# A two-layer gated cross-attention and mixture-of-experts kernel: unit slots of the second layer, the order before the first expert tile, and the place of a bias sum

## What is computed

```python
x = x + tanh(g_xattn[0]) * L0_xattn(layernorm(x), ctx)   # 16 heads of 16, 375 keys, clip, softmax, + bo
x = x + tanh(g_ffn[0])   * L0_ffn(layernorm(x))          # 8 experts, top 2, gelu; times three matrix exponentials; gated mix
x = x + tanh(g_xattn[1]) * L1_xattn(layernorm(x), ctx)   # 16 heads of 64, 371 keys, plus an attention over 4 more keys; LoRA weights
x = x + tanh(g_ffn[1])   * L1_ffn(layernorm(x))          # shared expert + 8 experts, top 2, silu gate
```

## Time and profile before

| | us |
|---|---|
| median of 3 runs | 988.82 (978.87, 988.82, 989.82) |
| the profiled execution | 985.29 |
| its span in the profile | 983.5 |
| PE, DVE, ACT, POOL busy | 861.8, 668.6, 497.5, 500.8 |
| mean granted TensorE clock | 0.945 of full speed |

### The profile page before, as it was taken

The page is one execution under the profiler, slowest core; times in us unless marked ns, Lnnn a source line. Parts: engine busy times, 40 slices in busy tenths (PEclk is TensorE's granted clock), DMA queues, the critical chain, the costliest instruction groups (busy, mean ns, idle before and its releaser), DMA issues.

```text
span 983.5 us, 21996 instructions
## 1 busy us (share of the span) xinstructions
PE 861.8 (88%) x7463; PEld 682.4 (69%) x7463; DVE 668.6 (68%) x1532; ACT 497.5 (51%) x1058; POOL 500.8 (51%) x525
## 2 busy tenths in 40 slices
PE   1789999999897999977679899898998976999994
PEld 1579988888775877755456677676776766666663
DVE  6487766666875768776657677777787777743333
ACT  4365555555533645542356655656556553334441
POOL 4779999998512324211126745556455562124420
PEclk9899999999856999998799999999999998999997
DMA  5423333347382225447002222222221248911114
GB/s 174 158 87 95 107 113 107 116 149 240 124 293 78 65 81 156 136 124 262 29 23 87 66 66 87 66 86 74 76 86 63 66 139 270 351 39 55 59 45 129
DMA packets 81485, 113.73 MB, mean 116 GB/s; under 512 B 7786, under 2 KB 60083, under 8 KB 81284
## 3 DMA queue, kind: packets, MB, share of 16 engines
q1 hardware_dynamic: 75556, 99.92, 32.0%
q0 software_dynamic: 4032, 11.02, 3.7%
q10 hardware_dynamic: 1824, 1.84, 0.5%
HBM read 75.78 MB, written 36.96 MB: 115 GB/s over the span
## 4 chain that ended last, share of the span: by engine, by line
PE 51%; DVE 15%; POOL 13%; issue 8%; ACT 6%; DMA 6%; SPq 0%; ACTq 0%; DVEq 0%; POOLq 0%
PE sp L892 5%; PE tp L906 5%; PE pb L850 5%; POOL Z L1296 4%; PE sp L2053 4%; PE tp L2053 3%; POOL Z L1304 3%; PE pb L2083 3%; POOL qz L1373 3%; PE tp L2278 3%; PE pb L871 3%; PE pb L844 3%; PE sp L1909 2%; ACT ST L1041 2%; PE pb L1927 2%
## 5 line engine op out<-in xcount | busy, mean ns | idle before, releaser
L1048 ACT ACTIVATE ST<-tp 125x672 f32<-125x672 f32 (+1 forms) x128 | 93.4, 730 | 156.3 <-PE tp L906 156.3
L892 PE MATMUL sp<-KT,qz 128*112 128x375 f16 (+1 forms) x768 | 118.5, 333 | 32.7 <-ACT ST L1041 21.2
L1296 POOL TENSOR_SCALAR Z<-Z 128x512 f32<-128x512 f32 x94 | 140.9, 1499 | 4.4 <-DMA Z<-in_moe 4.2
L906 PEld LDWEIGHTS tp<-identf,ST 112*125 112x125 f32 x768 | 98.5, 191 | 24.2 <-issue 14.3
L906 PE MATMUL tp<-identf,ST 112*125 112x112 f32 x768 | 111.6, 282 | 4.3 <-POOL ST L1404 3.3
L1304 POOL TENSOR_TENSOR Z<-Z 128x512 f16<-128x512 f32 x94 | 111.0, 1181 | 6.2
L892 PEld LDWEIGHTS sp<-KT,qz 128*112 128x112 f16 (+1 forms) x768 | 66.9, 129 | 63.7 <-ACT ST L1041 29.5
L1857 POOL DMA_INDIRECT back<-ST,slot_row x42 | 43.6, 1039 | 127.8 <-ACT ST L1967 67.1
L1851 POOL DMA_INDIRECT ST<-rows,slot_from x42 | 41.5, 988 | 93.6 <-DVE slot_weight L1836 52.7
L1177 DVE TENSOR_SCALAR_CACHE_REDUCE ST<-sp 112x375 f32<-112x375 f32 x128 | 65.0, 545 | 35.2 <-PE sp L892 35.1
L1404 POOL TENSOR_TENSOR ST<-pn,sums 112x8 f32<-112x8 f32 x64 | 12.9, 201 | 142.6 <-ACT ST L1041 142.6
(11 more groups left out here) (352 smaller groups left out, 1993.1 us busy)
## 6 DMA issues: line engine op xcount, KB each, us to landing
Z<-in_moe SPq DMA_DIRECT2D x86, 256.0 KB, 3.1
cut_scratch<-Z SPq DMA_DIRECT2D x86, 256.0 KB, 2.6
KT<-cut_scratch SPq DMA_DIRECT2D x16, 384.0 KB, 7.8
W<-cut_scratch SPq DMA_DIRECT2D x8, 512.0 KB, 5.6
W<-cut_scratch SPq DMA_DIRECT2D x32, 128.0 KB
W<-w_scratch SPq DMA_DIRECT2D x6, 512.0 KB, 8.8
V<-cut_scratch SPq DMA_DIRECT2D x8, 384.0 KB
own_scratch<-Z SPq DMA_DIRECT2D x8, 256.0 KB, 3.6
```

What stands on the lines that cost most here:

```text
L892: mm = pe.matmul(SB_[j][0:S, 0:L.keys], q, kT[bs % 2][qb][r, t, 0:L.keys], start=(n == 0), stop=(n == 2))
L906: mm = pe.transpose(TB_[j][0:CHUNK, c * S:(c + 1) * S], P_[:, st % 2, j, c * CHUNK:(c + 1) * CHUNK], identf[0:S, 0:S])
L1048: act.activation(PT[:, st % 2, :, 0, :] if l else PT0[:, st % 2, :, :], TP2[0:CHUNK, :, 0:NCH * S], ACT.Copy)\
L1296: pool.tensor_scalar(whole, whole, WS, None, ALU.mult).then_inc(s["cut_up"], 1)
```

## The change

- Layer 1's `at` becomes 0, 1, 2, ... 10, 12, ...: the second q unit goes from slot 2 to slot 1, each of the eight k units one slot earlier (3 to 10 become 2 to 9), the i unit from 11 to 10. The v units stay at 12, 13, 13, 14, 15, 15.
- `out_bias_gpsimd(0)` goes from the head of POOL's queue to behind `masks(1)`, and SP issues the two rows' transfers behind three of the late chunks.
- DVE before the first tile: `expm_first_vector`, then `bias_vector`, then `cut_x0_vector(0)`, then `expm_rest_vector` and `eyes_vector`.
- PE's transpose of the bias (`bias_turn_tensor`) is issued ahead of the last batch in `abel_tensor` and no longer after it.

```diff
-            at = dict(enumerate((0, 2, 3, 4, 5, 6, 7, 8, 9, 10, 11, 12, 13, 13, 14, 15, 15)))
+            at = dict(enumerate((0, 1, 2, 3, 4, 5, 6, 7, 8, 9, 10, 12, 13, 13, 14, 15, 15)))
...
-                out_bias_gpsimd(pool, 0)
                 masks(0, 0)
...
                         if b + 1 < B and n == pieces_by(b) + 2:
                             masks(b + 1, b + 1)
+                            if b == 0:
+                                out_bias_gpsimd(pool, 0)
...
+                if b == B - 1:
+                    bias_turn_tensor(pe)
...
-        def bias_tensor(pe):
-
+        def bias_turn_tensor(pe):
             pe.transpose(pb[0][0:E * NM, 0:128], b1[:, :, :].rearrange("p e m -> p (e m)"), identf[:, :])\
               .then_inc(s["bias_mm"], 1)
+
+        def bias_tensor(pe):
             pe.wait_ge(s["bias_set"], 1)
...
         def tiles0_vector(dve):
-            cut_x0_vector(dve, 0)
...
+            sp.wait_ge(s["chunk_lo"], 1)
+            chunks_sync(sp, NE, NE + 3)
             for l in range(2):
                 o = ROW[f"bo{l}"][0]
                 sp.dma_start(out_bias[:, l, :], a["rows"][0, o:o + C].partition_broadcast(S)).then_inc(s["w1_in"], 16)
-            sp.wait_ge(s["chunk_lo"], 1)
-            chunks_sync(sp, NE, NE + 3)
...
             owner_vector(dve, 0)
+            expm_first_vector(dve)
             bias_vector(dve)
-            expm_first_vector(dve)
+            cut_x0_vector(dve, 0)
             expm_rest_vector(dve)
```

## The result

| | median, us | ratio to the kernel before, 95% interval |
|---|---|---|
| before | 988.5 (978.9 to 996.0, 20 runs) | |
| after | 977.0 (972.4 to 985.3, 20 runs) | 0.989 [0.9871, 0.991] |

The changed kernel is 11.5 us faster by the medians, where 8.4 were forecast (980.4; range 972 to 990). Its profiled execution took 981.05 us, with a span of 979.3 and a mean granted clock of 0.936; the one of before took 985.29 at 0.945. So a difference of two whole spans says little here. I read stages from a mark at their start to a mark at their end, and compare whole times by medians and by the ratio only; the ratio gives 10.9 us. Some executions fall in a slower state and are left out of the ratios; one of them was profiled, the first of the kernel with both bias sums early, so that kernel is read from its second profile.

What follows compares the result with a forecast made beforehand. Layer 0's attention was bound by full PE and POOL, the stretch before the first tile by a chain of short steps. Terms -1.8 + 3.8 - 3.8 - 6.6 = -8.4 took the median 988.8 to 980.4 us; range 972 to 990.

Steps and rivals of the forecast that it cites:

- The bias sum leaves the start: Start of layer 0: without POOL's add, DVE's cut of WKV ends earlier and all behind it shifts, -1.8 us.
- It arrives in the first batch: Layer 0's first batch: DVE's 784-column cut waits for POOL's moved add, +3.8 us, bounds 0 and 4.5.
- My margin of 0.3 us: Layer 0's first batch: the add starts at about 52.8, DVE's 784-column cut 0.2 to 0.3 us after it.
- the add slips between the cuts: Rival, layer 0's first batch: the +3.8 falls away, so 976.6 us; chance 0.13.
- the two scalings: POOL's steps before the add, behind `masks(1)`: start at 50.8, take about 2 us.
- POOL's 6.5 us more: Layer 0, POOL's queue: 6.5 us more is covered by waits for q units, the longest shrinking to 2.5; cost 0.
- Before the first tile: Ahead of the first expert tile: DVE's new order and the early transpose start `up(0)` at 303.0 for 306.83, -3.8 us.
- the gather of 0.94 us: Before the first tile: a POOL gather beside L2308 in the old trace, read as showing no loss.
- The slots: Layer 1's seven batches: the q unit fills a wait, PE saves a k unit, -6.6 us, bounds 0 to -9.
- the t unit does not move: Layer 1's middle batch: the t unit stays at 636.39, so only one k unit, 0.80 us, is saved.
- start at 633.7 all the same: Layer 1's middle batch: `maxima(2)` on DVE can start at 633.7, with scores(2) at 632.3, 0.4 later.
- A mark that failed: Sign of being right: `up(0)` some 2 us earlier than 306.83 in absolute time.

Runs made afterwards that it cites:

- the move alone: The kernel before with only layer 0's bias sum moved behind `masks(1)`, with SP's order of transfers; ratio 1.0017 [0.9985, 1.0048].
- the two-source version: The changed kernel with the three scalings L2311 written as a product less its own source, two SBUF sources for one; ratio 0.9877 [0.9828, 0.9927].
- the early second sum: The changed kernel with the first bias sum ahead of `masks(2)` and layer 1's ahead of its batches; to the kernel before 0.9817, in a second series 0.9842.
- The separate ratios: The kernel before with one part changed each: slots alone 0.9899, the bias sum's move alone 1.0017, the order before the first tile alone 0.9941.

## Why the prediction was right, point by point

The forecast of a gain below 2% and the range held; 980.4 was 3.4 us too high.

*The bias sum leaves the start, -1.8.* Right: `masks(0)` starts at 28.32 us where it started at 29.96, 1.6 earlier.

*It arrives in the first batch, +3.8.* Right in mechanism, slightly over in size: the add began first, the cut grew by 4.11 - 0.95 = 3.16 us in the changed kernel and by 4.09 in the move alone. My margin of 0.3 us between the starts of add and cut was 1.2 and 0.3 in these two profiles. In the third with the sum in this place the cut came 1.8 us before the add, so there the rival "the add slips between the cuts" came half true: the 784-column cut slipped by and the next was held by 2.57 us. That two of three went my way is in part luck. The steps before it were off too: I had the two scalings start at 50.8, and they started at 48.20, directly behind `masks(1)`. The place was a bad one: ahead of `masks(2)` in POOL's queue the sum held no cut.

*POOL's 6.5 us more, 0.* Right in that the cover held, wrong in its number. I had the wait ahead of `masks(2)` shrink to 2.5 us; in the changed kernel the waits for q units between 66 and 130 us grew:

```profile
POOL qz L1373 <- DVE ST L1109: 10.6, 2, 8.0
```

The longest is 8.0 us, with the move alone it was 5.2, and in the two-source version POOL did not wait at all ahead of `masks(2)`. These starts scatter with the granted clock: `masks(2)` start at 79.57, 77.39 and 72.31 us in the three, and from 72.55 to 76.06 in six profiles whose layer 0 is that of the kernel before.

*Before the first tile, -3.8.* Right: 7.24 us against the forecast 7.5, 11.29 before, and by the steps I had: the scalings directly behind the owner table, L2297 done 5.10 us after it (forecast 5.4), the hi, the halving, 1.26 us later (forecast 1.24) `up(0)`. The one reading that failed is beside it. I took the gather of 0.94 us beside L2308 as proof of no loss; after the change the first two gathers' issues took 2.03 and 1.61 us and the first turn waited 0.95 us for its rows. The rule in the Trainium skill (SBUF — State Buffer, "Who interferes with whom") speaks of exactly this, and the trace agrees with it for the first gather, which ended 0.12 us after L2311. Its 0.84 us of loss lies under the 1.15 I allowed; the two together, 1.50, lie over it. I had also named the second and third gather; it was the first and second, because L2311 started 0.14 us after the owner table's last product and not 0.5. The loss was covered but for 0.15 us, because the hi stands behind ACT's L2297 anyway, which ended at 309.87. The late first turn ended at 309.88 and the hi started 5.15 us after the owner table. In the four profiles where the first turn ended early it started at 5.00, and `up(0)` came at 7.07 to 7.10 for 7.24. In one other profile (the early second sum, second time) the rows came a little later, the hi waited 0.24 us for the turn, and the stretch was 7.42. In the row of before, the gather had 0.5 us left when L2308 ended; that is the likely reason that it lost nothing, and it is not tested.

*The slots, -6.6.* Right in mechanism, under-sized. What I had for the middle batch came: the wait moved from scores(1) (0.20 left) to scores(2) (1.07, forecast 1.3), scores(6) waits for nothing at 651.60 (forecast 651.5), one k unit is saved. But a middle batch gains 1.14 us and not 0.8. The step that failed is "so the t unit does not move": from scores(1) to the t unit it is 636.48 - 627.79 = 8.69 us where it was 636.39 - 627.36 = 9.03. It waits for the cut of slot 4's k unit. That cut ended 8.98 us after scores(1) before (636.34) and ends 8.64 after it now (636.43), because `maxima(2)` in front of it moved too: it starts 5.85 us after scores(1) (633.64) where it was 6.41 (633.77). The second q unit's cut, 1.26 us long and 0.68 us of waiting for ACT ahead of it, no longer stands before it; a k unit's cut, 0.55 long, does. I had `maxima(2)` "start at 633.7 all the same", 6.3 after scores(1), behind a queue that I had not worked out again. That is 0.34, and 0.80 + 0.34 = 1.14. The first batch gains 0.47 in these two profiles (forecast 0.8), but kernels with the new slots scatter there from 36.69 to 39.84 and those without from 38.56 to 38.84, so its gain is not known. The wait of 1.02 ahead of its scores(6), which I had expected, is there:

```profile
529.74 1.18 PE L892 MATMUL sp<-KT,qz 64*112 64x371 f16 x6 [1.02 <-ACT ST L1041]
```

The second gains 1.50 (forecast 1.8), though kernels without the new slots scatter there, from 42.17 to 43.78, and those with them and the late second sum from 40.00 to 41.55. Together 0.47 + 1.50 + 5 x 1.14 = 7.7, of which only the last term is firm.

*The sum.* With measured terms: -1.6 + 3.2 - 4.05 - 7.7 = -10.2, for -11.5 by the medians. The rest is within the interval, which is 1.9 us to either side. The separate ratios add to -10.0 + 1.7 - 5.8 = -14.1 and so agree with the ratio's -10.9 only within their own intervals (3.7, 3.1 and 2.7 us to either side).

*A mark that failed.* I expected `up(0)` 2 us earlier in absolute time. It came 5.2 us later, because in the profiled execution layer 0 ended at 271.99 and not 262.61. Most of that is not the change: the two-source version has the same layer 0 and ended it at 261.89. See below.

## What to carry to other kernels

When a unit of work is moved into a wait, work out again every queue it was taken from, up to the next wait in the loop: here a q unit's cut that left DVE's queue gave 40% on top of the k unit saved. A big GpSimd instruction over SBUF should be put where GpSimd waits for others and VectorE has no two-source cut; in this kernel the first bias sum was worth about 4 us by its place alone, the second 0.5 us of wait and in most profiles another 1.5 with the clock. Two batches must be compared at the same granted clock before their difference is put down to an edit. And a row that shows no interference is evidence for its own overlap alone.

The best version measured has the new slots and order, the first bias sum ahead of `masks(2)` and the second ahead of layer 1's batches: 0.9817 [0.9774, 0.986] and 0.9842 [0.9799, 0.9884], medians 973.1 and 972.8 us.

## What the runs showed of the hardware

**TensorE's granted clock moves about in layer 0.** Busy time by stretch in the changed kernel, with the granted clock as the third number from the end:

```profile
40.00:50.00 10.00, 9.57 (x73) 8.09 (x72) 6.87 (x17) 6.79 (x12) 9.91 (x8) 0.92 0.32 97
50.00:60.00 10.00, 7.59 (x43) 6.42 (x41) 9.06 (x19) 4.59 (x7) 9.76 (x6) 0.76 0.00 0
60.00:70.00 10.00, 9.52 (x63) 8.79 (x61) 7.48 (x16) 5.18 (x8) 9.45 (x8) 0.73 0.43 129
70.00:80.00 10.00, 8.96 (x53) 7.48 (x53) 4.08 (x14) 3.63 (x7) 1.88 (x3) 0.61 0.28 84
80.00:90.00 10.00, 10.00 (x77) 9.06 (x76) 6.81 (x22) 5.14 (x10) 9.85 (x8) 0.88 0.01 2
```

In the kernel before, the first of them was 0.74 and the other four were 1.00. The version with slots and order alone, whose cut is not held, has 1.00 and 0.66 at 50 to 60 and 60 to 70; the one with the sum ahead of `masks(2)` 1.00 and 0.59. So the dip comes with and without the held cut. The end of layer 0 moves with it. In six profiles whose layer 0 is that of the kernel before, it lies from 262.61 us (1.00 from 50 to 90) to 268.81 (1.00, 0.61, 0.50, 0.87). Three with the changed kernel's layer 0 ended it at 271.99 (the rows above), 269.49 (0.80, 0.68, 1.00, 1.00) and 261.89 (0.89, 0.94, 1.00, 1.00). What sets the dip off is open.

**Where the clock is steady, a loop's period repeats to a few hundredths.** The third to sixth batches of layer 1 took 39.40 to 39.49 us in five kernels with the new slots that differ elsewhere (39.44 to 39.53 in the one with the early second sum), and 40.53 to 40.67 in five without. A stage's period is worth more here than twenty whole runs: it shows 1.14 us per batch where the interval of the total is 1.9 us to either side. That does not hold for the first two batches, where the clock is not steady.

**Gathers.** Undisturbed, the issue of the first took 1.19 us and of the others 0.95. Beside VectorE's scalings and products directly behind the owner table the first two took 2.03 and 1.61, and with two-source scalings 1.19 and 3.25.

**A large GpSimd add and VectorE's two-source cuts.** Beside the add of 4.5 us a cut of 512 columns took 2.46 us for 0.69, one of 784 took 4.11 and 5.04 for 0.95, one of 256 took 2.97 for 0.40. Each ended 0.3 to 0.9 us after the add.
